# A third slot for the prefix counts of a sorting stage: VectorE's copy of them waits for TensorE products of the set three back

## The reference, cut to what matters

```python
src, dst = edge_index[0], edge_index[1]                     # 100000 edges
gate = silu(edge_attr @ F1W + F1b) @ F2W + F2b              # one row of 48 for each edge
msg  = gate * h[dst] * (cw * mj)[:, None]
agg  = segment_sum(msg, src, num_segments=3125)
...                                                         # attention layers, three more networks
```

## Time and profile before

| what | us |
|---|---|
| time, median of 3 runs (lowest to highest) | 6147.38 (6138.8 to 6162.79) |
| span of the profiled execution | 6172.7 |
| `bucket`: first indirect DMA of a set of records | 137.17 |
| `bucket`: start of the last copy of L520 | 1204.54 |
| `bucket`: last indirect DMA ends | about 1371 |

### The profile page before, as it was taken

One profiled execution on the slowest core, in us unless ns is written; L12 is line 12 of the kernel. 1 busy time (PEld: TensorE's weight loads), 2 busy tenths in 40 slices (PEclk: granted clock), 3 DMA queues, 4 the chain that ended last, 5 costly groups with the idle time before them and its releaser, 6 DMA issues. The chain is left out here.

```text
span 6172.7 us, 186442 instructions
## 1 busy us (share of the span) xinstructions
PE 4389.3 (71%) x79347; PEld 3648.8 (59%) x79432; DVE 3821.1 (62%) x7925; ACT 2247.1 (36%) x7746; POOL 2684.3 (43%) x2702
## 2 busy tenths in 40 slices
PE   6676677725666479857985899489837765678887
PEld 3343344414555468846884788478835653677777
DVE  6555555538999767756774677477748335645244
ACT  3222222205666435543553455345520333300320
POOL 2666666666666346624662566256620340000000
PEclk7555555557999789968996999699959788788987
DMA  9222222227777344414331434144324626000000
GB/s 330 53 57 58 56 56 56 59 53 173 199 200 200 100 154 154 150 36 164 146 144 40 160 144 148 53 154 152 130 37 103 215 86 205 3 9 3 5 3 10
DMA packets 488183, 656.79 MB, mean 106 GB/s; under 512 B 316480, under 2 KB 370372, under 8 KB 484117
## 3 DMA queue, kind: packets, MB, share of 16 engines
q1 hardware_dynamic: 450965, 595.00, 30.7%
q0 software_dynamic: 33856, 48.44, 3.2%
q10 hardware_dynamic: 2496, 0.98, 0.1%
HBM read 464.16 MB, written 180.09 MB: 104 GB/s over the span
## 5 line engine op out<-in xcount | busy, mean ns | idle before, releaser
L299 POOL DMA_INDIRECT edges<-sb_bk_rec,sb_bk_pos x782 | 790.6, 1011 | 529.6 <-issue 224.1
L1681 ACT ACTIVATE sb_at_val<-banks,sb_at_prob 128x49 f32<-128x49 f32 x3800 | 773.5, 325 | 519.8 <-PE banks L1621 505.3
L1720 DVE TENSOR_REDUCE sb_at_tops<-banks 128x1 f32<-128x512 f32 x1000 | 626.0, 659 | 326.4 <-PE banks L1601 304.4
L1577 PE MATMUL banks<-sb_near,sb_at_hotT_d 128*128 128x49 bf16 x11100 | 618.8, 185 | 132.0 <-DMA sb_at_hotT_d<-rows_dst_t 65.5
L1535 POOL TENSOR_TENSOR sb_at_key<-sb_at_key,sb_at_attr 128x400 f32<-128x400 f32 (+1 forms) x400 | 371.0, 928 | 714.4 <-ACT sb_at_key L1665 622.1
L1577 PEld LDWEIGHTS banks<-sb_near,sb_at_hotT_d 128*128 128x128 fp8e4 x11100 | 567.1, 97 | 137.3 <-issue 70.7
L1579 PE MATMUL banks<-sb_queryp,sb_at_hotT_s 128*128 128x49 bf16 x11400 | 634.9, 186 | 16.4 <-issue 16.3
L1579 PEld LDWEIGHTS banks<-sb_queryp,sb_at_hotT_s 128*128 128x128 fp8e4 x11400 | 565.7, 96 | 18.9 <-issue 18.6
L1598 PE MATMUL banks<-sb_at_hotT_s,sb_off 128*128 128x512 fp8e4 x1000 | 374.4, 374 | 113.2 <-DVE sb_at_tops L1720 111.3
L1542 POOL TENSOR_TENSOR sb_at_val<-sb_at_val 128x490 f32<-128x490 f32 (+1 forms) x400 | 387.1, 968 | 67.7 <-ACT sb_at_val L1681 66.5
L1544 POOL TENSOR_TENSOR sb_at_val<-sb_at_val 128x490 f32<-128x490 f32 (+1 forms) x400 | 386.1, 965 | 31.3
(11 more groups left out here) (690 smaller groups left out, 10689.2 us busy)
## 6 DMA issues: line engine op xcount, KB each, us to landing
sb_at_attr<-attr SPq DMA_DIRECT2D x100, 760.0 KB, 7.0
sb_at_hotT_s<-rows_src_t SPq DMA_DIRECT2D x100, 608.0 KB
sb_at_hot_s<-rows_src SPq DMA_DIRECT2D x100, 608.0 KB
sb_at_hotT_d<-rows_dst_t SPq DMA_DIRECT2D x100, 592.0 KB
edges<-sb_pad SPq DMA_DIRECT2D x95, 460.0 KB
sb_gt_rec<-edges SPq DMA_DIRECT2D x25, 1748.0 KB
sb_we_hotT<-rows_dst_t SPq DMA_DIRECT2D x52, 592.0 KB, 3.9
attr<-sb_gt_rec SPq DMA_DIRECT2D x25, 760.0 KB
```

The source lines that it names most:

```text
L299: pool.indirect_dma_start(list1, bass.IndirectOffsetOnAxis(pos[:, t:t + 1], 0), rec[:, k, j, :], None).then_inc(sent[k], 16)
L1577: pe.matmul(ps[:, 0, H1 * j:H1 * j + H1], where, what, start=(n == 0), stop=(n == 2))
L1681: ins = act.mul(val[:, v % VB, j, 0, :], ps[:, 5, H1 * j:H1 * j + H1], prob[:, i % 2, k:k + 1])
L1720: dve.tensor_reduce(tops[:, i % 2, g:g + 1], ps[:, 3 + x % 2, 0:P * len(RG[g])], AX, ALU.max).then_inc(s_top, 1)
```

## The change

`pre` gets three slots in place of two. `before(s)` now writes slot `s % 3`, and waits for `s_ahead` of set s - 3; `cross` and `ahead` index the slots in the same way. On no engine does an instruction move, appear or go away. What is different in the instruction streams is the size of the first `memset` of `pre` (37x1275 elements for 37x850), the addresses, and the value that L520 waits for (set 2 no longer waits for `s_ahead` at all).

```diff
+    SLOTS = 3
...
-    pre = m.sb("bk_pre", [NW, 2, S1, NB], BF16)
+    pre = m.sb("bk_pre", [NW, SLOTS, S1, NB], BF16)
...
                 if g == 0:
                     pe.wait_ge(s_pre, s + 1)
-                    pe.matmul(bank[:, 0:NB * S1], c["identb"][0:NW, 0:NW], along(pre[:, (s + 1) % 2, SET, :], S1), start=True,
+                    pe.matmul(bank[:, 0:NB * S1], c["identb"][0:NW, 0:NW], along(pre[:, (s + SLOTS - 1) % SLOTS, SET, :], S1), start=True,
                               stop=False)
...
                 for t in range(SET):
-                    ins = pe.matmul(ps[:, 2, NB * t:NB * t + NB], hT[0:NW, s % TR, P * t:P * t + P], pre[:, s % 2, t, :],
+                    ins = pe.matmul(ps[:, 2, NB * t:NB * t + NB], hT[0:NW, s % TR, P * t:P * t + P], pre[:, s % SLOTS, t, :],
                                     start=True, stop=True)
...
             def before(s):
                 dve.wait_ge(s_cross, s + 1)
-                if s >= 2:
-                    dve.wait_ge(s_ahead, s - 1)
-                dve.tensor_scalar(pre[:, s % 2].rearrange("p t b -> p (t b)"), ps[0:NW, 1, 0:NB * S1], 255.0, None, ALU.min
+                if s >= SLOTS:
+                    dve.wait_ge(s_ahead, s - SLOTS + 1)
+                dve.tensor_scalar(pre[:, s % SLOTS].rearrange("p t b -> p (t b)"), ps[0:NW, 1, 0:NB * S1], 255.0, None, ALU.min
                                   ).then_inc(s_pre, 1)
```

## The result

| | before | changed |
|---|---|---|
| median of 4 runs each, us (lowest to highest) | 6143.09 (6134.46 to 6162.79) | 6228.26 (6213.66 to 6232.84) |
| ratio, with its 95% interval | | 1.0131 (1.0115 to 1.0146) |
| span of the profiled execution, us | 6172.7 | 6231.2 |

The change makes the kernel slower, by 85 us. The forecast was 6131 us, with a range from 6096 to 6160: the time lies outside it and on the other side. The lines of the changed kernel have numbers one higher than those of before (the copy is L521, the indirect DMA L300, ScalarE's two copies L441 and L448).

The account below looks back on a forecast made before the run. The prediction took a 25.3 us loop closing over GpSimd's indirect DMAs, with TensorE handing over late, as the bound. 14.0 us over 40 sets plus 2.6 at the start made 16.6 us: 6147.4 to 6131 us, range 6096 to 6160.

Parts of the forecast that it names:

- What bounds the kernel: A 25.3 us loop over GpSimd's DMAs, VectorE's copy and first record; TensorE hands over `cross` late, after GpSimd's run.
- The gain in a single set: VectorE's copy no longer waits from `cross` to `ahead`: 0.35 us a set, 14.0 us over 40 sets, period 24.97 us.
- The mark for `cross`: ScalarE's L447 start, 0.35 us before VectorE's copy, taken as when the `cross` signal comes; bounds 0 and 1.16 us.
- the first rival: On TensorE the `cross` signal comes about with that of L329's transposes: 1.16 us a set, 49 us, 6098 us; chance 0.10.
- The start: GpSimd's third set starts sooner, as the copy of set 8 loses its wait: 2.6 us.
- What was hidden and is next: `ranks` needing `ahead`, and TensorE's identity product L337 with 0.35 us of idle time used up: costs nothing.
- The edits costed at nothing: Longer fill of `pre` (0.77 to 1.15 us, hidden behind GpSimd's padding wait) and 850-byte slots in VectorE's copy: no cost.
- GpSimd runs two sets without a pause: Record ready before GpSimd's set ends, so TensorE cannot clear: 5.1 us per two sets, 20 times, 6249 us; chance 0.07.
- the recorded end being true: `cross` on TensorE usable at its recorded end, so the copy goes at 764.1: 175 us gained, 5972 us; chance 0.04.
- No gain: Signals of `cross` and `ahead` come together, or TensorE is late in turn, or its order holds VectorE: 6147 us; chance 0.13.

Follow-up runs that it names:

- the run from set 12 on: Changed kernel with the old wait on the copy for the first twelve sets, the new one from set 12: 6221.38 us, before 6134.27, ratio 1.0143.
- the hold on the records: Changed kernel, but VectorE waits for `ahead` of the same pass before writing the records: 6130.02 us, before 6160.02, ratio 0.995; elsewhere 1.001 to 1.0019.

## Why the prediction was wrong, point by point

**What bounds the kernel: right.** The recorded end of `cross` is no time at which anyone could go on. The changed kernel has many passes in which results that TensorE has ended by its rows reach ScalarE much later: the transposes of 784.57 to 786.98 were copied at 818.41. The Trainium skill's sentence ("Perfetto Trace Analysis", section "Summary: the profiler window per engine type"), by which the passing on of the semaphore is hidden behind an estimated end, holds here too.

**The gain in a single set: right only inside a regular loop.** In the regular passes from 561 to 661 us the period is 24.97, to the hundredth what was forecast. But GpSimd's idle time is 4.06 us, not 4.3, and its DMAs take a little longer; the agreement of the sum is partly luck.

**The mark for `cross`: mis-sized.** I took 0.35 us from ScalarE's L447 and a bound of 1.16 us from its L440, each in the regular loop of before, where all signals came at once after GpSimd's run. The 1.16 is too low even there: it is set 31's, one of only six of the 40 passes in which the last transposes reached ScalarE so close to the copy. In the other 34 they came 1.8 to 4.0 us ahead of it, 2.04 on average over all 40, so that the bound and the first rival should have had some 82 us in place of 46. And the bounds held for that state alone. Where `cross` comes while GpSimd still runs, as in the run from set 12 on, the first copy with the new wait came 3.75 us sooner than the last with the old one. With it goes the sentence that 2.68 + 1.93 us of lead are "far from" a gain of 0.35 or 1.16: 3.75 us less turned a lag of 2.33 us into a lead of 1.42, and a lead of 1.93 - 0.30 = 1.63 us is all that it takes for GpSimd to go on with its usual 0.30; with 1.42 it idled 0.76.

**The step that failed** is this one: "The delayed hand-over is tied to the end of its run, so the next `cross` signal also comes 0.35 us sooner, and the whole loop shrinks to 24.97 us." It takes for granted that GpSimd may start its run sooner and everything follows. But hand-over during a run isn't nothing and isn't tied to its end; it goes on slowly, and how far TensorE is when the run starts decides when the next signals come. In the changed kernel the run starts before the pass is handed over, as the timeline of a regular pass shows:

```profile
584.23 0.59 DVE L521 TENSOR_SCALAR sb_bk_pre<-banks 37x425 bf16<-37x425 f32 x1 [4.71 <-remote]
...
586.15 0.97 POOL L300 DMA_INDIRECT edges<-sb_bk_rec,sb_bk_pos  x1 [4.06 <-DVE sb_bk_rec L514]
...
586.74 0.60 PE L362 MATMUL banks<-sb_bk_pre,sb_bk_hT 37*128 37x25 bf16 x16
...
587.84 0.54 PE L338 MATMUL banks<-sb_bk_pre,sb_ident_bf 37*37 37x425 bf16 x1
```

`ahead` runs at 586.74, 0.59 us after GpSimd's start, and the identity product 3.61 us after the copy. Before, `ahead` had ended at 773.59, 2.19 us ahead of GpSimd's start, and the identity product came 0.65 us after the copy. I had read the idle 9.76 us of VectorE's copy as a wait of which only 0.35 us counted, and costed the rest at nothing, because it was covered. I should have asked what the wait orders: a record may not be written before `ahead` of its pass has been handed over, only because it stands behind the copy. That order was not meant, and it kept the loop regular.

**The start: not borne out.** I had given it 2.6 us. In this trace the third set came 8.9 us sooner, but that can't be put down to the change: in the traces with late hand-over the third set starts at 184.04 and 195.16 with the changed kernel, and with the old wait at 192.95 (before) and 186.22 (the run from set 12 on). The start differs by more from run to run than the term was worth. What was gained here was used up by the tenth set: set 9 starts at 370.57, where before had it at 370.18.

**"What was hidden and is next": wrong for TensorE.** I saw that the identity product had 0.35 us to give, and said that GpSimd's start doesn't hang on when TensorE begins its next pass. That is so, and it is just the trouble: GpSimd moved ahead of TensorE, and nothing made it wait.

**The edits costed at nothing: right as far as seen.** The copy takes 0.59 to 0.60 us with three slots; the memset and the slots don't show in any ratio.

**The rivals.** "GpSimd runs two sets without a pause" is what happened. Its mechanism was right, so was the point from which it decides (the record is there before the last DMA is out), and the sign of it that was named, passes of two lengths. Its price was put at 5.1 us for two sets; measured were 58.9 - 50.7 = 8.2. That it would happen "20 times" was too much, since regular passes lie between: eight such pairs, a ninth that begins with an idle time of 1.27 us, and seven passes of 27 to 30 us beside them. The 6249 us that it gave were nearer than everything else, by two errors against each other. With 0.07 it had far too low a chance. Its condition was tied to the recorded end being true, but a slow hand-over during the run was enough; the earlier trace rows had shown exactly this run of two sets in the kernel before, where the hand-over was late as well. "No gain" had said that TensorE might be late in turn; it was, but this did not cancel the gain, it led to the loss.

## What to carry to other kernels

A wait that looks like a pure stall may be the only thing that keeps another engine's start in order. Before relaxing it, list what is issued behind it on its engine and whom that releases, and ask whether the released engine may now run ahead of one that is slow; if so, put a hold where that start is issued and relax only the rest. Here both together gave 0.995 where relaxing alone gave 1.013 to 1.015.

A margin read from a loop in its steady state holds for that state, and its bound has to be taken from all passes, not from the one whose rows were printed (here 2.04 us on average, for 1.16). If the change moves the state, look for the place in the trace where the loop was once in the other one, here the first two sets of GpSimd.

## What the runs showed of the hardware that was not expected

- While GpSimd issues indirect DMAs one after the other (0.97 us each, 0.30 between), TensorE in the late condition comes, from some 10 us into the run on, to start an instruction only every 0.7 or 1.4 us (from 784.57 in the run that began at 773.11), and others get its results up to some 31 us after its recorded end (transposes of about 787, copied at 818.41). It clears within some 4 us once GpSimd pauses.
- The same kernel, before, took 6134 to 6160 us in some comparisons and 5911 to 5930 us in others, some 3.8% apart, and one chip showed both. In `bucket`, with prompt hand-over a set takes 21.0 us and GpSimd is the bound, with late hand-over 25.3; over 40 sets that is 172 us of the difference of some 225. The rest wasn't followed.
- A change may have opposite signs in the two: this one 1.013 to 1.015 and 0.9985; the hold on the records 0.995 and 1.001 to 1.002.

Two things stay open. Why TensorE hands over late, and in some comparisons only. The traces of the late condition hold about a quarter fewer records of semaphore changes than the others (45.5 to 47.6 thousand against some 62, with all the DMAs in), and these are missing where the indirect DMAs are: between 200 and 700 us before has 2.4 thousand and the changed kernel with prompt hand-over 10.4, while from 2000 to 4000 us both have some 17 thousand. The run with a quarter of the DMAs, from a comparison with late hand-over, has 5.3 thousand between 200 and 700 us. The missing records may be a cause, such as the recording itself being congested, or a result; which, no run shows. And how the drift builds up from one regular pass to the next, until the copy comes ahead of GpSimd's end: the passes from 561 to 661 us were stable for four sets and then broke without a row that says why, and in the second run of the changed kernel with late hand-over it was six, from 975.99 us on.
